# One Trainium2 core, a graph network: ScalarE's work on a tile put in another order

## The chip, the cores and the metric

The kernel runs on one core of one Trainium2 chip. The metric is the device time of one execution in microseconds (us). Before the change it was 12189.33 us, the median of 3 runs (12188.68 to 12192.55).

## The reference, cut to what matters

Four graph layers run over 6250 nodes of 128 features with 206,250 directed edges (self loops among them): a graph attention layer made of two attention convolutions, a neighbour sum, a transformer-like attention and an edge network. The change touches the two attention convolutions (4 heads of 32) of the first layer:

```python
h = (x @ W).reshape(N, H, C)
e = leaky_relu(alpha_s[src] + alpha_d[dst], 0.2)
e_exp = exp(e - segment_max(e, dst)[dst])
alpha = e_exp / (segment_sum(e_exp, dst)[dst] + 1e-16)
out = segment_sum(h[src] * alpha[:, :, None], dst)
...
feat_neigh = segment_sum(edge_val[:, None] * feat_in[edge_col], edge_row)   # second layer
```

The neighbour sum of the second layer is computed as a dense matrix product. That dense matrix of edge weights is written to DRAM beside the two convolutions, half of its columns in each.

## The kernel before, in words

**Nodes and units.** The nodes are sorted by falling degree into 49 tiles of 128, and the tiles into NB = 7 bands of B7 = 7. The edges into a band are cut into units. A unit is S = 2 edge slots for each of the band's 7 x 128 nodes, so 14 gathers of 128 table rows. Empty slots gather one and the same dummy row. The program has 130 units in all. A band has between 15 and 29 of them, and `k.beside` deals them out to its seven tiles.

**The attention pass** (`attention_pass`) is called three times: twice by `gat_conv` (called pass 1 and pass 2 here), and once for the later attention layer, without the dense rows. Its engines are these:

- POOL issues the gathers (L818) into a ring of RU = 4 units. Before a unit it claims `used` (the ring place is free again) and, before every second unit, the index that SP loads (L832).
- SP tells DVE by `landed` that a unit has arrived, and loads the next index once two units have arrived.
- DVE takes a unit in `unit`: scores (L1289, L1291), the running maximum (L1136), the difference `x` (L1137) with `e_ready`. It then waits for `p_ready`, multiplies the gathered rows by the exponentials (L1143 twice, where the second frees the ring place), rescales the sum (L1147) and adds (L1150, L1151).
- ScalarE answers each `e_ready` with the exponential (L1205) and a copy of the maximum (L1207).

**The dense rows** (`DenseRows`, in pass 1 and pass 2 only) are built tile by tile between the units. A tile has two phases, and in this program each phase has one chunk (`nch` is 1 everywhere). In a phase, DVE writes two sets of 16 one-hot blocks of 128x128 (L937, L939) from a small fetched column `col`. ScalarE first issues the fetch of the column for later use (`act_fetch`, L969, two DMAs) and then multiplies the 16 blocks `hot_lo` by the edge weights (L993). PE multiplies the pairs into four PSUM banks (L961), which it has cleared before with a product of zeros (L954). PE increments `full` when a phase is done. ScalarE's `act_store` waits for `full` and for `stage_out` (its store before has landed), copies the four banks to SBUF (L1004), giving each back to PE by `bank_free`, and issues two DMAs of 512 KB to DRAM (L1008). There is one set of four banks, so PE's products of phase 1 begin after the copies of phase 0.

**Order of DVE's work on a tile:** phase 0, phase 1, in pass 2 one step of the sums below, then the tile's units (2 to 5), and at the end of a band the division and, in pass 2, a layer norm.

**Sums over sources** (`SourceSums`, pass 2 only, from the second band on): the dense rows of the band before are read back in 14 parts of 1568 KB (`act_load`, L1042, two per tile, issued by ScalarE as the first thing of a tile and each only when `mat_free` says that PE is done with the buffer), multiplied by PE (`pe_step`, L1054, two groups of 7 products per tile, after the tile's second phase) and added by DVE (L1064, `dve_step`).

**Order of ScalarE's work on a tile, before:** the two loads (pass 2), phase 0, store 0, phase 1, all exponentials of the tile, store 1.

Of the kernel before, what the change touches and what calls it, by code (L numbers as in the profile page):

```python
# [15 lines left out]
ALU = mybir.AluOpType  # L16
ACT = mybir.ActivationFunctionType
AX = mybir.AxisListType
RMAX = bass.bass_isa.ReduceOp.max
ds = bass.ds  # L20
# [3 lines left out]
E = 206250  # L24
# [5 lines left out]
B7 = 7  # L30
NB = T // B7
W7 = B7 * P
S = 2
# [4 lines left out]
CROWS = EROWS + 16  # L38
DCOLS = 256
DROWS = -(-E // DCOLS)  # L40
UMAX = E // S + 256
SCOLS = UMAX * UG + 8 * CH * B7
SPARTS = ((0, 44), (44, 88), (88, P))
TROWS = 2 * EROWS + T + 16
# [144 lines left out]
def order_nodes(k, dst_rows, dst_firsts):  # L189
# [3 lines left out]
    with ExitStack() as st:  # L193
# [22 lines left out]
        band, bcnt, run = (s.sb(n, [P, NB]) for n in ("band", "bcnt", "run"))  # L216
        bi = s.sb("bi", [P, NB], I32)
# [47 lines left out]
        def _(dve):  # L265
# [86 lines left out]

            c(dve.tensor_scalar(bi[:, :], band[:, :], float(S - 1), None, ALU.add))
            c(dve.tensor_single_scalar(bi[:, :], bi[:, :], 1, ALU.arith_shift_right))
            c(dve.tensor_scalar(bcnt[:, :], bi[:, :], float(B7), None, ALU.max))
            c(dve.tensor_tensor_scan(run[:, :], k.ones[:, 0:NB], bcnt[:, :], 0.0, ALU.mult, ALU.add))
            c(dve.tensor_scalar(ti[:, 0:1], run[:, NB - 1:NB], 1.0, None, ALU.add))
            c(dve.tensor_single_scalar(ti[:, 0:1], ti[:, 0:1], 2, ALU.arith_shift_right))
# [512 lines left out]


def band_units(k, eng, b):
    return eng.value_load(k.units[0:1, ds(b, 1)], min_val=B7, max_val=UMAX)


def band_start(k, eng, b):
# [190 lines left out]
def attention_pass(k, table, slot_src, width, heads, dim, scores, start, finish, extra, beside=None, spill=None,  # L1068
# [6 lines left out]
    with ExitStack() as st:  # L1075
# [45 lines left out]
        def _(dve):  # L1121
# [32 lines left out]
            def band(b, before):  # L1154
                start(dve, c, b * B7, acc, e[:, S, :], work, second)
                c.reset()
                u0 = band_start(k, dve, b)
                if rows_of is None:
                    with dve.Fori(u0, u0 + band_units(k, dve, b)) as u:
                        unit(u)  # L1160
                else:
                    run.put(u0)
                    for w in range(B7):
                        rows_of.dve_tile(dve, rows_of.chunks(dve, b * B7 + w))
                        if before and w:
                            by_source.dve_step(dve, w - 1)
                        many = dve.value_load(k.beside[0:1, ds(b * B7 + w, 1)], min_val=1, max_val=UMAX)
                        u = run.value()
                        with dve.Fori(u, u + many) as v:
                            unit(v)  # L1170
                        run.advance(many)
                if before:
                    by_source.dve_step(dve, B7 - 1)
                c(dve.drain())

                a4 = acc[:, :, :].rearrange("p w (h c) -> p (w h) c", h=heads)
                c(dve.tensor_scalar(rden[:, :], a4[:, :, dim], 1e-16, None, ALU.add))
                c(dve.reciprocal(rden[:, :], rden[:, :]))
                done = k.out[:, ds(b * B7, B7), :] if by_source is None else by_source.xs[:, :, :]
                c(dve.tensor_tensor(done.rearrange("p w (h c) -> p (w h) c", h=heads),  # L1180
                                    a4[:, :, 0:dim], rden[:, :].unsqueeze(2).broadcast_to([P, HW, dim]), ALU.mult))
                finish(dve, c, b * B7, done, by_source)
                c.reset()
# [13 lines left out]
        @block.scalar  # L1197
        def _(act):
            act.activation(warm[:, :], k.ones[:, 0:1], ACT.Exp)

            def exponents(n):
                with act.Fori(0, n):
                    act.wait_ge(e_ready, 1)
                    act.sem_clear(e_ready)
                    act.activation(p, x[:, :, :], ACT.Exp)  # L1205

                    act.activation(e[:, S, :], newmax[:, :], ACT.Copy).then_inc(p_ready, 1)  # L1207

            def band(b, before):
                for w in range(B7):  # L1210
                    t = b * B7 + w
                    if before:
                        if w == 0:
                            act.wait_ge(rows_of.stage_out, 32)
                        by_source.act_load(act, b - 1, w)
                    n = rows_of.chunks(act, t)
                    for u in range(rows_of.PHASES):
                        rows_of.act_phase(act, t, u, n)
                        if u < rows_of.PHASES - 1:
                            rows_of.act_store(act, t, u)  # L1220
                    exponents(act.value_load(k.beside[0:1, ds(t, 1)], min_val=1, max_val=UMAX))
                    rows_of.act_store(act, t, rows_of.PHASES - 1)

            if rows_of is None:
                exponents(act.value_load(k.total[0:1, 0:1], min_val=2, max_val=UMAX))
            else:
                rows_of.act_begin(act, spill)
                if by_source is None:
                    with act.Fori(0, NB) as b:
                        band(b, False)  # L1230
                else:
                    band(0, False)
                    with act.Fori(1, NB) as b:
                        band(b, True)
                rows_of.act_end(act)
                if by_source is not None:
                    for w in range(B7):
                        by_source.act_load(act, NB - 1, w)
# [1413 lines left out]
```

## Time and profile before

| | us |
|---|---|
| median of 3 runs | 12189.33 |
| the profiled execution's own time | 12168.16 |
| its span, first to last instruction | 12166.3 |
| pass 1, first dense-row work to the last unit | 418 to 2826 |
| pass 2, likewise | 2954 to 5634 |
| third attention pass | 5998 to 8320 |

Engines overlap, so their busy shares don't add up to the span. A wait "for DVEq" or "POOLq" means that the engine's own sequencer held it: it stood at a semaphore or ran control instructions. "issue" is a gap with no wait that the trace shows. An "x16" in a timeline joins that many instructions of a kind that follow each other.

### The profile page before, as it was taken

Reading aid. Unit: us, or ns where it says so; the run is one execution under the profiler, and the core shown is the slowest. Engines: PE = TensorE matmul, PEld = TensorE weight load, DVE = VectorE, ACT = ScalarE, POOL = GpSimd, SP = SyncE. Lnnn points to the kernel's source line nnn. Section 1 sums busy time; section 2 is a strip of 40 time slices with the busy share of each in tenths; the row PEclk is TensorE's granted clock in tenths of the full one; section 3 lists DMA queues with packets and bytes.
Section 4 is the critical chain, followed back from the end, with each engine's and each line's share of the span. In section 5 each row is a group of like instructions: output and inputs, shape, how many; then the busy total and the mean of one; then the engine's idle time right before and its main releaser. Section 6 shows DMA issues by size and latency. Waiting matters only on the chain. (4 is left out here: it accounts for less than half of the span.)

```text
span 12166.3 us, 91441 instructions
## 1 busy us (share of the span) xinstructions
PE 3704.8 (30%) x14114; PEld 2564.3 (21%) x14213; DVE 6446.5 (53%) x10684; ACT 2415.0 (20%) x6031; POOL 7481.0 (61%) x7840
## 2 busy tenths in 40 slices
PE   2212233332224555555200000003311111113987
PEld 2212222322113333333200000001211111112433
DVE  6445666664545665563655666665332222223877
ACT  1112333331212233221100000000000000001876
POOL 4676777774767766552576777772276777774023
PEclk7556666665557777778655555556655555556999
DMA  2255444443375665555247444442137333334866
GB/s 59 68 76 92 101 107 108 114 109 58 89 102 150 167 163 160 151 156 144 75 111 103 112 112 112 112 112 35 40 103 92 104 104 107 104 107 122 280 243 214
DMA packets 928552, 1422.94 MB, mean 117 GB/s; under 512 B 191108, under 2 KB 723306, under 8 KB 927992
## 3 DMA queue, kind: packets, MB, share of 16 engines
q0 software_dynamic: 277904, 662.94, 26.4%
q10 hardware_dynamic: 549664, 498.96, 14.4%
q1 hardware_dynamic: 100680, 257.93, 6.3%
q14 instruction: 229, 1.88, 0.0%
q8 instruction: 75, 1.23, 0.0%
HBM read 1064.18 MB, written 355.03 MB: 117 GB/s over the span
## 5 line engine op out<-in xcount | busy, mean ns | idle before, releaser
L818 POOL DMA_INDIRECT ring<-gat_table,index x3640 | 3470.8, 954 | 1536.9 <-issue 1054.2
L818 POOL DMA_INDIRECT ring<-b_table,index x1820 | 1730.2, 951 | 671.0 <-issue 526.0
L818 POOL DMA_INDIRECT ring<-kv_table,index x1820 | 1722.8, 947 | 594.6 <-issue 526.1
L961 PE MATMUL pairs<-hot_lo,hot_hi 128*128 128x128 f32 x6272 | 1173.9, 373 | 1845.9 <-PEq L959 1845.9
L961 PEld LDWEIGHTS pairs<-hot_lo,hot_hi 128*128 128x128 f32 x6272 | 1142.3, 286 | 1922.0 <-issue 1922.0
L993 ACT ACTIVATE hot_lo<-hot_lo,wt 128x128 f32<-128x128 f32 x3136 | 949.4, 387 | 1895.4 <-ACTq L991 1881.5
L1911 DVE TENSOR_TENSOR tb<-bt,att 128x1792 f32 x130 | 263.2, 2025 | 1661.7 <-DVEq L106 1661.7
L1143 DVE TENSOR_TENSOR first<-ring,first 128x924 f32<-128x924 f32 x260 | 292.5, 1125 | 1495.6 <-DVEq L106 1495.6
L1933 PE MATMUL bt<-ident,ring 128*128 128x128 f32 x1820 | 417.2, 421 | 1932.0 <-PEq L106 1932.0
L2066 ACT ACTIVATE r<-kept_ring,coef 128x448 f32<-128x448 f32 x1040 | 763.8, 758 | 184.9 <-ACTq L106 161.0
L713 PE MATMUL tp<-ident,stage 128*128 128x128 f32 x196 | 49.0, 427 | 2444.7 <-DVEq L700 2410.5
L1933 PEld LDWEIGHTS bt<-ident,ring 128*128 128x128 f32 x1820 | 370.2, 226 | 1979.2 <-issue 1979.2
L1744 DVE TENSOR_TENSOR ring<-ring,qt 128x1904 f32 x130 | 277.9, 2138 | 786.5 <-DVEq L106 786.5
L954 PE MATMUL pairs<-nil 128*128 128x512 bf16 x686 | 277.5, 439 | 1317.6 <-PEq L106 1283.9
L1054 PE MATMUL fsum<-layer_out,xs 128*128 128x448 f32 x1372 | 540.6, 546 | 71.8 <-PEq L1052 70.2
L937 DVE TENSOR_TENSOR hot_hi<-hi,ramp 128x512 f32<-128x512 f32 x784 | 542.7, 692 | 29.4 <-DVE hi L931 3.2
L713 PEld LDWEIGHTS tp<-ident,stage 128*128 128x128 f32 x196 | 37.9, 222 | 2456.0 <-issue 2456.0
L939 DVE TENSOR_TENSOR hot_lo<-lo,ramp 128x512 f32<-128x512 f32 x784 | 550.1, 702 | 0.0
L2369 POOL TENSOR_SCALAR lift<-fnt,coef,bound 128x896 f32<-128x896 f32 x7 | 23.5, 3361 | 767.7 <-issue 518.6
L1205 ACT ACTIVATE p<-x 128x168 f32<-128x168 f32 x130 | 40.8, 314 | 2261.5 <-DVE x L1137 2261.5
L2020 ACT ACTIVATE v<-v,ep 128x1 f32<-128x1 f32 x2 | 0.6, 294 | 2392.5 <-DVEq L2013 2392.5
L1004 ACT ACTIVATE dstage<-pairs 128x512 f32<-128x512 f32 x784 | 404.8, 602 | 327.6 <-ACTq L1002 327.6
(414 smaller groups left out, 7926.4 us busy)
## 6 DMA issues: line engine op xcount, KB each, us to landing
kept_ring<-kept SPq DMA_DIRECT2D x260, 896.0 KB, 4.6
dense_weights<-dstage ACTq DMA_DIRECT2D x392, 512.0 KB
layer_out<-dense_weights ACTq DMA_DIRECT2D x98, 1568.0 KB, 14.8
kept<-tb ACTq DMA_DIRECT2D x132, 896.0 KB, 3.8
ring<-gat_table,index POOLq DMA_INDIRECT x3640
ring<-kv_table,index POOLq DMA_INDIRECT x1820
ring<-b_table,index POOLq DMA_INDIRECT x1820
col<-turned ACTq DMA_DIRECT2D x400, 32.0 KB
```

The lines of the kernel that those rows point to most:

```text
L818: pool.indirect_dma_start(self.ring[:, r * UG + i, :], None, self.table, bass.IndirectOffsetOnAxis(self.index[:, half, at:at + 1], 0)).the ...
L937: dve.tensor_tensor(self.hot_hi[:, u, four, :], self.hi[:, four].unsqueeze(2).broadcast_to(shape), ramp, ALU.is_equal)
L939: dve.tensor_tensor(self.hot_lo[:, u, four, :], self.lo[:, four].unsqueeze(2).broadcast_to(shape), ramp, ALU.is_equal).then_inc(self.marke ...
L954: pe.matmul(self.ps[:, b, :], self.nil[:, 0:P], self.nil[:, :], start=True, stop=False, skip_group_check=True)
L961: mm = pe.matmul(self.ps[:, b, i * P:(i + 1) * P], self.hot_hi[:, u, 4 * b + i, :], self.hot_lo[:, u, 4 * b + i, :], start=False, stop=Fal ...
L993: last = act.activation(self.hot_lo[:, u, j, :], self.hot_lo[:, u, j, :], ACT.Copy, scale=self.wt[:, u, j:j + 1])
L1004: act.activation(self.stage[:, 4 * b:4 * b + 4, :].rearrange("p i c -> p (i c)"), self.ps[:, b, :], ACT.Copy).then_inc(self.bank_free[b], 1)
L1054: mm = pe.matmul(self.ps[:, u, 0:BLK], self.xs[:, j, :], self.mat[:, u, j, :], start=(j == 0), stop=(j == B7 - 1))
L1143: ins = dve.tensor_tensor(by_head(dst), by_head(got[:, part, 0:VB]), weight[:, part, :].unsqueeze(3).broadcast_to([P, B7, heads, dim + 1]) ...
L1744: return (lambda: dve.tensor_tensor(keys4, keys4, qt[:, :, :].unsqueeze(1).broadcast_to([P, S, B7, VB]), ALU.mult), lambda: dve.tensor_red ...
L1933: mm = pe.transpose(bt[:, r % 2, q, w * P:(w + 1) * P], ga.ring[:, r * UG + q * B7 + w, :], k.ident[:, :])
L2066: act.activation(self.r4[:, q, :], self.slots[:, r, q * QW:(q + 1) * QW], ACT.Relu, bias=self.coef[:, 1:2], scale=self.coef[:, 0:1]).then_ ...
```

## The change

ScalarE now does, for a tile: the two loads (pass 2), phase 0, phase 1, one exponential, store 0, the other exponentials, store 1. Since the exponential is now once outside of the loop and the rest inside, every tile must have at least two units, so the floor of a band's units goes from 7 to 14. The smallest band has 15 units in the trace, and the total stays 130. UMAX, a bound for allocation, grows by 256.

```diff
-UMAX = E // S + 256
+UMAX = E // S + 512
...
-            c(dve.tensor_scalar(bcnt[:, :], bi[:, :], float(B7), None, ALU.max))
+            c(dve.tensor_scalar(bcnt[:, :], bi[:, :], float(2 * B7), None, ALU.max))
...
-            def exponents(n):
-                with act.Fori(0, n):
-                    act.wait_ge(e_ready, 1)
-                    act.sem_clear(e_ready)
-                    act.activation(p, x[:, :, :], ACT.Exp)
-
-                    act.activation(e[:, S, :], newmax[:, :], ACT.Copy).then_inc(p_ready, 1)
+            def exponent():
+                act.wait_ge(e_ready, 1)
+                act.sem_clear(e_ready)
+                act.activation(p, x[:, :, :], ACT.Exp)
+
+                act.activation(e[:, S, :], newmax[:, :], ACT.Copy).then_inc(p_ready, 1)
...
                     for u in range(rows_of.PHASES):
                         rows_of.act_phase(act, t, u, n)
-                        if u < rows_of.PHASES - 1:
-                            rows_of.act_store(act, t, u)
-                    exponents(act.value_load(k.beside[0:1, ds(t, 1)], min_val=1, max_val=UMAX))
-                    rows_of.act_store(act, t, rows_of.PHASES - 1)
+                    exponent()
+                    rows_of.act_store(act, t, 0)
+                    many = act.value_load(k.beside[0:1, ds(t, 1)], min_val=2, max_val=UMAX)
+                    with act.Fori(1, many):
+                        exponent()
+                    rows_of.act_store(act, t, 1)
```

The value bounds of two other loads are adapted to the new floor.

## Rows read from the trace of the kernel before

**Rows 1.** The page, group of the gathers of pass 1 and pass 2

```profile
L818 POOL DMA_INDIRECT ring<-gat_table,index x3640 | 3470.8, 954 | 1536.9 <-issue 1054.2
```

**Rows 2.** Waits of POOL (total, times, longest), 1972 to 2826 us (pass 1)

```profile
POOL ring L818 <- issue: 180.0, 588, 1.1
POOL ring L818 <- POOLq L106: 26.9, 39, 4.6
```

**Rows 3.** Waits of POOL, 3549 to 5634 us (pass 2, after its first gather-heavy band)

```profile
POOL ring L818 <- POOLq L106: 297.5, 67, 24.6
```

**Rows 4.** Timeline (start, length, instruction, idle before), DVE: last waits for a gather

```profile
1954.62 0.22 DVE L1289 TENSOR_TENSOR es<-ring,ad 128x56 f32<-128x56 f32 x1 [7.39 <-DVEq L106]
...
3525.13 0.22 DVE L1289 TENSOR_TENSOR es<-ring,ad 128x56 f32<-128x56 f32 x1 [1.38 <-DVEq L106]
```

**Rows 5.** Timeline, ScalarE, a tile of two units in pass 2

```profile
4685.24 0.22 ACT L1205 ACTIVATE first<-x 128x84 f32<-128x84 f32 x1
...
4692.85 2.06 ACT L1004 ACTIVATE dstage<-pairs 128x512 f32<-128x512 f32 x4
...
4707.27 4.78 ACT L993 ACTIVATE hot_lo<-hot_lo,wt 128x128 f32<-128x128 f32 x16 [12.36 <-ACTq L991]
...
4717.69 1.57 ACTq L1008 DMA_DIRECT2D dense_weights<-dstage  x2
4720.93 2.67 ACTq L969 DMA_DIRECT2D col<-turned  x2
4723.74 4.78 ACT L993 ACTIVATE hot_lo<-hot_lo,wt 128x128 f32<-128x128 f32 x16 [6.26 <-ACTq L991]
4728.43 0.22 ACT L1205 ACTIVATE first<-x 128x84 f32<-128x84 f32 x1
```

**Rows 6.** Timeline, PE, the same tile

```profile
4694.45 5.50 PE L1054 MATMUL fsum<-layer_out,xs 128*128 128x448 f32 x14 [0.41 <-PEq L1052]
...
4716.15 1.84 PE L954 MATMUL pairs<-nil 128*128 128x512 bf16 x4 [1.01 <-PEq L106]
4725.16 6.74 PE L961 MATMUL pairs<-hot_lo,hot_hi 128*128 128x128 f32 x32 [7.16 <-PEq L959]
```

**Rows 7.** Windows (busy per engine, then PEclk, DMA share, GB/s): that product's start

```profile
4725.00:4728.00 3.00, 2.84 (x13) 2.87 (x14) 0.00 (x0) 3.00 (x12) 0.00 (x0) 0.50 0.22 74
```

**Rows 8.** DMA traffic, 4716 to 4732 us in 40 slices of 0.4 us

```profile
GB/s 44 0 98 76 0 65 109 49 178 179 164 175 164 189 140 270 298 246 228 184 200 280 308 261 127 16 0 0 0 0 8 12 14 2 0 0 0 0 0 0
```

**Rows 9.** Timeline, ScalarE, a tile of three units in pass 2

```profile
4772.53 0.22 ACT L1205 ACTIVATE first<-x 128x84 f32<-128x84 f32 x1
...
4787.36 2.06 ACT L1004 ACTIVATE dstage<-pairs 128x512 f32<-128x512 f32 x4
...
4802.08 4.79 ACT L993 ACTIVATE hot_lo<-hot_lo,wt 128x128 f32<-128x128 f32 x16 [12.65 <-ACTq L991]
...
4822.10 0.22 ACT L1205 ACTIVATE first<-x 128x84 f32<-128x84 f32 x1
```

**Rows 10.** Timeline, ScalarE, first exponentials of two tiles in pass 1, two units between them

```profile
1545.25 0.22 ACT L1205 ACTIVATE first<-x 128x84 f32<-128x84 f32 x1
...
1582.70 0.22 ACT L1205 ACTIVATE first<-x 128x84 f32<-128x84 f32 x1
```

**Rows 11.** Timeline, ScalarE and POOL, end of the first band in pass 1

```profile
904.87 4.78 ACT L993 ACTIVATE hot_lo<-hot_lo,wt 128x128 f32<-128x128 f32 x16 [46.10 <-ACTq L991]
946.22 2.07 ACT L1004 ACTIVATE dstage<-pairs 128x512 f32<-128x512 f32 x4 [36.57 <-ACTq L1002]
...
959.36 0.22 ACT L1205 ACTIVATE first<-x 128x84 f32<-128x84 f32 x1
...
962.90 0.94 POOL L818 DMA_INDIRECT ring<-gat_table,index  x1 [39.93 <-POOLq L106]
```

**Rows 12.** Timeline, SP and DVE, end of pass 1

```profile
2791.67 1.07 SPq L832 DMA_DIRECT2D index<-slot_src  x3
...
2824.45 1.12 DVE L1151 TENSOR_TENSOR acc<-first,acc 128x924 f32<-128x924 f32 x1
```

More of the change, by code:

```diff
@@ L873, in band_units @@
 def band_units(k, eng, b):
-    return eng.value_load(k.units[0:1, ds(b, 1)], min_val=B7, max_val=UMAX)
+    return eng.value_load(k.units[0:1, ds(b, 1)], min_val=2 * B7, max_val=UMAX)
 def band_start(k, eng, b):
@@ L1166, in band @@
                             by_source.dve_step(dve, w - 1)
-                        many = dve.value_load(k.beside[0:1, ds(b * B7 + w, 1)], min_val=1, max_val=UMAX)
+                        many = dve.value_load(k.beside[0:1, ds(b * B7 + w, 1)], min_val=2, max_val=UMAX)
                         u = run.value()
@@ L1218, in band @@
                         rows_of.act_phase(act, t, u, n)
-                        if u < rows_of.PHASES - 1:
-                            rows_of.act_store(act, t, u)
-                    exponents(act.value_load(k.beside[0:1, ds(t, 1)], min_val=1, max_val=UMAX))
-                    rows_of.act_store(act, t, rows_of.PHASES - 1)
+                    exponent()
[4 more added lines that the diff above has]
+                    rows_of.act_store(act, t, 1)
             if rows_of is None:
-                exponents(act.value_load(k.total[0:1, 0:1], min_val=2, max_val=UMAX))
+                with act.Fori(0, act.value_load(k.total[0:1, 0:1], min_val=2, max_val=UMAX)):
+                    exponent()
             else:
```

## The prediction

> **What bounds the kernel now.** I read the page first, then windows and waits for each attention pass, then the timelines of the engines. The page names POOL: 3640 gathers of 954 ns in pass 1 and pass 2 [rows 1]. With the 0.31 us that follow each (180.0 over 588, [rows 2]) a gather costs 1.26 us, a unit of 14 gathers 17.6 us, and that is POOL's pace: 35.3 us for a tile of two units, 52.9 for three. Averages hide who is last, so the next question is who waits for whom. DVE waits for a gather for the last time at 1954.62 in pass 1, and at 3525.13 in pass 2 [rows 4]. From there to the end of either pass (2826 and 5634) the gathers are there before DVE wants them, and POOL waits for DVE: 26.9 us in the last three bands of pass 1, 297.5 us in pass 2 from 3549 on, the usual 0.31 us each included [rows 2, 3]. So 850 us of pass 1 and 2085 us of pass 2 are not set by POOL. The third pass has no dense rows and is not touched.
>
> What DVE waits for there is the tile's first exponential. DVE is ready for it some 10 us early in pass 1 and 13 to 16 us in pass 2, since ScalarE comes to it only after store 0 and phase 1. I call its start T. From T to T a tile of two units takes 37.45 us in pass 1 [rows 10] and 43.19 us in pass 2 [rows 5], one of three units in pass 2 49.57 us [rows 9]. POOL would need 35.3 and 52.9. In pass 2 the 36 steps between tiles of one band from 3549 on divide into 20 of two units (mean 43.2), 10 of three (mean 50.3) and 6 in which a DMA issue of ScalarE is held up (48.8 to 61.8), so the rows shown are typical.
>
> **The direct effect.** Between the end of phase 0's blocks (4707.27 + 4.78 = 4712.05) and the start of phase 1's (4723.74) ScalarE spends 11.69 us: it waits for PE, copies four banks, issues the store and then the fetch [rows 5]. After the change what stays is the control code before the fetch (4720.93 less the store's end 4719.26: 1.67), the fetch 2.67 and 0.14 more: 4.48 us. The first exponential comes 7.21 us earlier after the same start of phase 0. Nothing else is removed. The two store DMAs, the copies and the second fetch are all still issued, and the code of one more exponential per tile costs no time that the rows show.
>
> **Pass 1, the pace.** The loop there runs from T over DVE's two units (about 15 us) to the next phase 0 and back: 37.45 less 7.21 is 30.2. ScalarE's own loop is now longer, because PE begins phase 1's products only after the copies: copies at T + 0.4, zeros done at T + 3.0 (the copies begin 0.74 us before the first zeros, which take 1.84, [rows 6]), products until T + 9.9 (below), copies of store 1 until T + 13, its DMAs until T + 15, control code 1.7. So phase 0's fetch starts at T + 17 instead of T + 15 (1560.24 by the timeline), and the loop is 32.5 us. That is under POOL's 35.3, so POOL's gathers become the bound of pass 1. Its end moves: POOL loses its waits (26.9 less 39 x 0.31 = 14.8 us), so the last index load, which follows the landing of the last units, goes from 2791.67 to 2777 [rows 12]. DVE then needs about 8 us for the last unit and is done at 2785 instead of 2825.57: **40 us** gained. The bounds are 0 (the loop stays over 35.3) and 54 (the landing itself, held up by gathers of the dummy row, comes earlier still).
>
> **The end of the first band.** Gathers of the dummy row fill the DMA engines there. Store 0 waits until 946.22 for the landing of the store before, the first exponential comes at 959.36, and POOL stands 39.93 us until 962.90 [rows 11]. After the change the exponential doesn't wait for that landing. With 4.48 us between the phases it comes at about 909.65 + 4.48 + 4.7 = 919. But store 0 is then next, and the second exponential stands behind it until 946.22 + 2.07 + 1.57 + 1.7 = 951.6. The ring place of the first unit comes free in time and that of the second at 954. POOL, which also needs an index that lands late, gains about 20 us, and DVE, whose five units end about 8 us after a chain that starts at 951.6 instead of 959.97 plus one unit, gains about 15. Low bound 8 (the fetch is blocked until 946 as well), high 27. Pass 1 follows POOL: **20**. Pass 2 has the same event and follows DVE: **15**.
>
> **Pass 2, the pace.** Here PE closes a second loop. Its step of the sums comes after phase 1's products, and the second load of the next tile, which stands ahead of phase 0 on ScalarE, waits for the end of that step. Before, the step ended at 4699.95 and phase 0's blocks began 7.32 us later, T + 22.03 [rows 5, 6]. After: zeros done at T + 3.0, 0.3 for the loop's start, products 6.6, then 0.4 + 5.5 + 0.4 + 5.5 for the two groups of the step: T + 21.7, and phase 0's blocks at T + 29.0. From there to T again it was 43.19 - 22.03 = 21.16 and is now 13.95. The loop is **42.95 us** where it was 43.2: of the 7.2 us, 7.0 are given back. In a tile of three units ScalarE was held by the third exponential anyway (copies at T + 14.83, blocks at T + 29.55, [rows 9]) and PE is done by T + 21.7, so nothing is given back and 50.3 becomes about 43. The first tile of a band starts from DVE, and gains 7.2 less 0.5, since the last step of the band before now ends 1 us later.
>
> Sum: 20 x 0.25 = 5; 10 x 7.3 = 73; 6 x 6.7 = 40; the six held steps 15 (one of three units, one with a store issue in front of the exponential): **130 us** (133 rounded). POOL's 297.5 us of waits show that it can follow.
>
> The products' 6.6 us are the least certain. They took 6.74 at the lower clock level of 1.2 GHz (granted 0.50, [rows 7]), with PE idle for 7.16 us before [rows 6], but paced by ScalarE. All blocks now stand ready. At the lower level I keep near that row; the bound below is half of it, 3.4 us, at 2.4 GHz. The Trainium skill, "TensorE: Matmul & The Clock Gate", section "HAM oscillation — how this bites in real kernels", says that a PE which idles between bursts starts each burst at the lower clock; that speaks for the long value and against the change, and this trace agrees with 0.50. By it the sum stays as it is.
>
> Store 1's copies wait for store 0's landing. Traffic ends at about 4726.4, 8.7 us after the issue at 4717.69 [rows 8], so it lands at T + 11.4, and the loads are ready before T + 21.7 all the same. A landing of over 13 us would lengthen the loop.
>
> **Sum.** 40 + 20 + 15 + 130 = 205 us. The profiled execution's own time is 12168.16, 21 us under the median, and would be 11963. The median goes from 12189.33 to **11985 us**.
>
> **Rivals.**
> - *PE comes up early.* Phase 1's products run at the upper clock level, right behind the zeros. The loop of pass 2 is 3.3 us shorter in 33 steps: 109 us more, **11876**. For it: the products now join the step in one run. Against: 7 us of idling before. 15 in 100.
> - *More is given back.* Store 0 and store 1 are 9 us apart instead of 18, and the loads follow at once; DMA issues stall ScalarE as in the six held steps. 2 us more in 33 steps and half of the 40 us lost at the end of pass 1: 86 us less, **12070**. 18 in 100.
> - *The gathers are the bound.* POOL is the busiest engine; if all waits of DVE are slack the time stays at **12189**. Against: no wait for a gather after 1954.62 and 3525.13. 7 in 100.
> - *Slower.* The second exponential now stands behind store 0. ScalarE is free at T + 0.4 + 2.1 + 0.2 + 1.6 + 1.7 = 6.0 and DVE asks at T + 7.0, so there is 1 us of room. A store that stalled 5 us, by a landing or a full queue, would cost 4 us in each of the 63 tiles that DVE or ScalarE sets: 252 less 205, **12236**. From 4.3 us on it eats the gain. Against: the landing in 8.7 us. 5 in 100.
>
> **Numbers.** The forecast has 55 in 100, with 11930 to 12035 as its own range. The range over the first three is 11865 to 12095. A difference under 0.2% (24 us) can hardly be told from none. Faster by more: 0.88; within: 0.07; slower: 0.05.
>
> **What would show it.** In pass 1, DVE's waits for gathers (L1289) come back after 1954 and the wait ahead of L1143 turns into them; the last unit ends some 60 us earlier. In pass 2 the distance between first exponentials is near 43 in tiles of two and of three units alike, ScalarE's second load starts at about T + 22, and the products of phase 1 take 6 to 7 us right behind the zeros. If that distance is below 40, PE was sized wrongly; if above 45, the loads or stores stall; if store 0 starts late, the second exponential moves with it.

## The result and the profile after

The changed kernel takes **11841.72 us** (median of 4 runs, 11837.08 to 11864.19) beside 12189.01 us of the kernel before (4 runs, 12181.88 to 12192.55). The ratio is 0.9719, its 95% interval 0.9703 to 0.9736: 2.8% faster, where 1.7% was forecast. The time lies 23 us under the low end of the range. The profiled execution took 11864.19 us and its span is 11862.3, 304.0 less than the span before. It was the slowest of its four, 22 us over their median, and the one before lay 21 us under its median, so the traces show some 43 us less of a difference than the medians. In lines of the changed kernel the exponential is L1204 (L1205 before), the copy behind it L1206 (L1207) and the first read of a gathered unit L1291 (L1289); the variants below move these and other lines by up to five more.

I read first how long POOL was held at its gathers in the whole program, because the gathers were the busiest group and the forecast left them with slack. The columns are the total in us, the number of waits and the longest. Before:

```profile
POOL ring L818 <- POOLq L106: 695.6, 406, 78.1
```

After:

```profile
POOL ring L818 <- POOLq L106: 368.6, 409, 78.0
```

Nearly the same number of waits lasts 327 us less, and the saving is 347 us: what was won is for the most part the time that POOL had stood still. The page after, groups of POOL and DVE in pass 1 and pass 2:

```profile
L818 POOL DMA_INDIRECT ring<-gat_table,index x3640 | 3477.4, 955 | 1204.2 <-issue 1046.9
...
L1143 DVE TENSOR_TENSOR first<-ring,first 128x924 f32<-128x924 f32 x260 | 292.6, 1126 | 559.6 <-DVEq L106 552.7
...
L1291 DVE TENSOR_TENSOR es<-ring,ad 128x56 f32<-128x56 f32 x260 | 56.1, 216 | 947.3 <-DVEq L106 947.3
```

The same two groups of DVE before:

```profile
L1143 DVE TENSOR_TENSOR first<-ring,first 128x924 f32<-128x924 f32 x260 | 292.5, 1125 | 1495.6 <-DVEq L106 1495.6
...
L1289 DVE TENSOR_TENSOR es<-ring,ad 128x56 f32<-128x56 f32 x260 | 57.0, 219 | 326.4 <-DVEq L106 326.4
```

DVE's wait for the exponential (ahead of L1143) fell from 1495.6 to 559.6 us, and its wait for a gathered unit rose from 326.4 to 947.3. A gather costs what it did (955 ns, 954 in [rows 1]), and its idle time fell from 1536.9 to 1204.2. Of what is left, 1046.9 stands under "issue", the 0.3 us behind each gather. Pass 2 after its first gather-heavy band shows it most clearly. Waits of POOL, 3494 to 5302 us, the stretch that was 3549 to 5634 before:

```profile
POOL ring L818 <- POOLq L106: 19.5, 64, 0.3
```

Of 297.5 us [rows 3] 19.5 are left, and no wait is longer than 0.3 us. One line of the view that groups instructions, POOL, 3494 to 5230 us:

```profile
L818 POOL DMA_INDIRECT ring<-gat_table,index x1378 | 1315.8, 955 | 420.2 <-issue 400.7 <-POOLq L106 19.5
```

Busy and idle time add up to the whole 1736 us: 1378 gathers at 1.26 us each, one behind the other. The issue of the gathers is now the bound of pass 2 from 3494 to POOL's last gather at 5234. The 67 us from there to the end of the pass are not POOL's: they belong to the last units, of which more below. DVE tells the same from the other side, in pass 2 (3494 to 5320 us):

```profile
DVE first L1143 <- DVEq L106: 291.6, 99, 24.0
DVE es L1291 <- DVEq L106: 140.0, 20, 14.7
```

and in pass 1 (1958 to 2770 us):

```profile
DVE es L1291 <- DVEq L106: 172.6, 22, 17.2
DVE first L1143 <- DVEq L106: 42.2, 45, 2.3
```

L1291 is the wait for a gathered unit. Before, there was none in the like stretches (behind 1954.62 and 3525.13, [rows 4]). In pass 1 the wait for the exponential (L1143) has shrunk to 2.3 us at most, from up to 22.1 before. The last unit of pass 1 begins its product at

```profile
2771.26 1.13 DVE L1143 TENSOR_TENSOR first<-ring,first 128x924 f32<-128x924 f32 x1 [0.74 <-DVEq L106]
```

in the timeline after and is finished 5.5 us later, at 2776.8, where it was 2825.57 [rows 12]: 48.8 us. The last unit of pass 2 ends at 5302.0, where it was 5632.9: 330.9 us. So pass 2 itself gave 282 us. Three parts make it up, read by taking the same gather in both traces. The end of the first band put POOL 17 us ahead (46.7 us ahead of the old kernel in front of it, 63.7 behind it). From there to POOL's last gather (5580.35 before, 5233.77 now) it won 283 us, of which its waits are 278 (297.5 less 19.5). Behind the last gather some 16 us were lost again: the pass ended 51.6 us after it before and ends 67.3 us after it now.

**One tile of two units in pass 2.** The timeline of ScalarE, beside [rows 5]:

```profile
4826.59 0.22 ACT L1204 ACTIVATE first<-x 128x84 f32<-128x84 f32 x1
...
4826.87 2.02 ACT L1004 ACTIVATE dstage<-pairs 128x512 f32<-128x512 f32 x4
4829.10 1.57 ACTq L1008 DMA_DIRECT2D dense_weights<-dstage  x2
4833.74 0.24 ACT L1204 ACTIVATE first<-x 128x84 f32<-128x84 f32 x1 [4.86 <-DVE x L1137]
...
4837.27 2.06 ACT L1004 ACTIVATE dstage<-pairs 128x512 f32<-128x512 f32 x4 [3.14 <-ACTq L1002]
4839.53 1.42 ACTq L1008 DMA_DIRECT2D dense_weights<-dstage  x2
4841.38 6.28 ACTq L1042 DMA_DIRECT2D layer_out<-dense_weights  x2
4849.28 3.40 ACTq L969 DMA_DIRECT2D col<-turned  x2
4852.82 2.44 ACT L993 ACTIVATE hot_lo<-hot_lo,wt 128x128 f32<-128x128 f32 x8 [13.49 <-ACTq L991]
4855.17 0.48 ACTq L969 DMA_DIRECT2D col<-turned  x1
...
4855.74 0.56 ACTq L969 DMA_DIRECT2D col<-turned  x1
4855.76 6.53 ACT L993 ACTIVATE hot_lo<-hot_lo,wt 128x128 f32<-128x128 f32 x22
4862.18 0.24 ACT L1204 ACTIVATE first<-x 128x84 f32<-128x84 f32 x1
```

From T to T it is 35.59 us, not 42.95. The reader should look at L969 near 4855: the fetch for phase 1 is issued while the blocks of phase 0 still run, and there is no gap between the 16 blocks of one phase and those of the other. The first exponential comes 9.36 us after the start of phase 0 (4852.82 to 4862.18), not 13.95. So it is in nearly all tiles of pass 2 from the second band on, but for the first of each band. In most tiles of pass 1 it is 11.23 us: there the second 16 blocks start 1.37 us behind the first, because DVE has only just written its first set of phase 1 (ready at 1547.89, ScalarE starts at 1548.03). PE beside it [rows 6]:

```profile
4827.58 2.02 PE L954 MATMUL pairs<-nil 128*128 128x512 bf16 x4 [2.87 <-PEq L106]
4829.40 5.77 PE L961 MATMUL pairs<-hot_lo,hot_hi 128*128 128x128 f32 x32
4835.58 5.50 PE L1054 MATMUL fsum<-layer_out,xs 128*128 128x448 f32 x14 [0.41 <-PEq L1052]
4841.48 5.50 PE L1054 MATMUL fsum<-layer_out,xs 128*128 128x448 f32 x14 [0.41 <-PEq L1052]
```

The step ends at T + 20.4 (forecast 21.7), and the blocks follow 5.84 us later (forecast 7.32). PE's clock during the zeros and the products, in windows (the granted clock is the column before the DMA share):

```profile
4827.50:4829.40 1.90, 1.82 (x4) 0.55 (x5) 1.90 (x3) 1.38 (x3) 1.60 (x2) 0.50 0.32 73
4829.40:4831.40 2.00, 2.00 (x11) 2.00 (x11) 1.97 (x2) 0.00 (x0) 1.39 (x3) 0.50 0.50 114
...
4833.40:4835.20 1.80, 1.77 (x15) 1.58 (x13) 1.06 (x2) 0.39 (x2) 1.32 (x2) 0.94 0.97 252
```

Zeros and products begin at 1.2 GHz (0.50) after 2.87 us without work; until 4826.5 the granted clock had been 1.00. The last products run near 2.4 GHz (0.94).

**The end of the first band in pass 1**, timeline of ScalarE, beside [rows 11]:

```profile
869.32 33.09 ACTq L969 DMA_DIRECT2D col<-turned  x2
902.55 2.44 ACT L993 ACTIVATE hot_lo<-hot_lo,wt 128x128 f32<-128x128 f32 x8 [39.62 <-ACTq L991]
...
915.02 0.22 ACT L1204 ACTIVATE first<-x 128x84 f32<-128x84 f32 x1
...
949.34 2.07 ACT L1004 ACTIVATE dstage<-pairs 128x512 f32<-128x512 f32 x4 [33.95 <-ACTq L1002]
951.61 4.34 ACTq L1008 DMA_DIRECT2D dense_weights<-dstage  x2
956.75 0.24 ACT L1204 ACTIVATE first<-x 128x84 f32<-128x84 f32 x1 [5.34 <-DMA raw<-in_edges_dram,rid]
```

The first exponential no longer waits for the landing (915.02, before 959.36), and the second does: it stands behind store 0 until 956.75. Later, in the sixth tile of the last band of pass 2, a store's issue itself took long:

```profile
5207.71 26.99 ACTq L1008 DMA_DIRECT2D dense_weights<-dstage  x2
5235.49 0.24 ACT L1204 ACTIVATE first<-x 128x84 f32<-128x84 f32 x1 [27.99 <-DMA raw<-in_edges_dram,rid]
```

From T to T this tile takes 76.4 us, where it took 52.3 before. The tile ahead of it had been held before (59.7 us, by a store's issue of 11.06 and a fetch of 8.86) and takes 37.6 now, so over both tiles the loss is 2 us (114.0 beside 112.0). Such a hold can still cost time there, because it lasts past POOL's last gather at 5234. The releaser in brackets, a DMA long past, is only inferred; what ended just before the exponential is the store's issue, ahead of it in ScalarE's order.

### The profile page after: what moved, and what is told of

It is laid out like the page before. It is cut to its first block and busy times, and to the rows that moved or that the text cites. A ratio compares the mean times of both kernels' runs of the same rounds, so it can differ in the third digit from the quotient of the medians.

```text
span 11862.3 us, 91343 instructions
## 1 busy us (share of the span) xinstructions
PE 3664.7 (31%) x14212; PEld 2474.3 (21%) x14213; DVE 6449.6 (54%) x10684; ACT 2409.2 (20%) x6031; POOL 7496.8 (63%) x7840
## 5 line engine op out<-in xcount | busy, mean ns | idle before, releaser
L818 POOL DMA_INDIRECT ring<-gat_table,index x3640 | 3477.4, 955 | 1204.2 <-issue 1046.9
L961 PE MATMUL pairs<-hot_lo,hot_hi 128*128 128x128 f32 x6272 | 1069.8, 350 | 997.7 <-PEq L959 981.9
L961 PEld LDWEIGHTS pairs<-hot_lo,hot_hi 128*128 128x128 f32 x6272 | 1049.9, 265 | 1059.9 <-issue 1049.2
L954 PE MATMUL pairs<-nil 128*128 128x512 bf16 x784 | 359.0, 531 | 1833.6 <-PEq L106 1753.1
L1143 DVE TENSOR_TENSOR first<-ring,first 128x924 f32<-128x924 f32 x260 | 292.6, 1126 | 559.6 <-DVEq L106 552.7
L1291 DVE TENSOR_TENSOR es<-ring,ad 128x56 f32<-128x56 f32 x260 | 56.1, 216 | 947.3 <-DVEq L106 947.3
L937 DVE TENSOR_TENSOR hot_hi<-hi,ramp 128x512 f32<-128x512 f32 x784 | 544.4, 694 | 29.4 <-DVE hi L931 3.2
L954 PEld LDWEIGHTS pairs<-nil 128*128 128x128 bf16 x784 | 80.2, 102 | 2072.7 <-issue 2067.2
L1204 ACT ACTIVATE p<-x 128x168 f32<-128x168 f32 x130 | 40.8, 314 | 2275.6 <-DVE x L1137 2275.6
```

What stands on the lines that cost most here:

```text
L818: pool.indirect_dma_start(self.ring[:, r * UG + i, :], None, self.table, bass.IndirectOffsetOnAxis(self.index[:, half, at:at + 1], 0)).the ...
L937: dve.tensor_tensor(self.hot_hi[:, u, four, :], self.hi[:, four].unsqueeze(2).broadcast_to(shape), ramp, ALU.is_equal)
L954: pe.matmul(self.ps[:, b, :], self.nil[:, 0:P], self.nil[:, :], start=True, stop=False, skip_group_check=True)
L961: mm = pe.matmul(self.ps[:, b, i * P:(i + 1) * P], self.hot_hi[:, u, 4 * b + i, :], self.hot_lo[:, u, 4 * b + i, :], start=False, stop=Fal ...
L1143: ins = dve.tensor_tensor(by_head(dst), by_head(got[:, part, 0:VB]), weight[:, part, :].unsqueeze(3).broadcast_to([P, B7, heads, dim + 1]) ...
```

## The experiments

All ratios are to the kernel before, timed on the same chip in the same series; 0.001 is 12 us.

| | median, us | ratio | 95% interval |
|---|---|---|---|
| the change | 11841.72 | 0.9719 | 0.9703 to 0.9736 |
| floor_only | 12195.99 | 1.0001 | 0.9992 to 1.0011 |
| pass1_only | 12115.68 | 0.9962 | 0.9949 to 0.9976 |
| pass2_only | 11889.29 | 0.9773 | 0.9760 to 0.9787 |
| drain_pass1 | 11841.40 | 0.9713 | 0.9697 to 0.9729 |
| drain_pass2 | 11878.51 | 0.9742 | 0.9725 to 0.9758 |
| store_first | 11910.54 | 0.9771 | 0.9755 to 0.9788 |
| short_step_old | 12138.11 | 0.9981 | 0.9971 to 0.9990 |
| short_step | 11802.59 | 0.9702 | 0.9686 to 0.9718 |
| split_loads | 11808.06 | 0.9710 | 0.9693 to 0.9726 |
| two_stages | 11811.54 | 0.9712 | 0.9698 to 0.9725 |
| two_stages_split | 11793.77 | 0.9696 | 0.9683 to 0.9709 |
| two_stages_short | 11790.05 | 0.9680 | 0.9667 to 0.9694 |

**floor_only**: the kernel before with the new floor of units and the new bounds alone.

```diff
-            c(dve.tensor_scalar(bcnt[:, :], bi[:, :], float(B7), None, ALU.max))
+            c(dve.tensor_scalar(bcnt[:, :], bi[:, :], float(2 * B7), None, ALU.max))
```

> The kernel before with nothing but the new floor of two units per tile and the larger bound UMAX. All theories: no tile changes its units, the time stays within 0.2% of 12189 us. Rival D: part of the gain is from another dealing of units, over 25 us faster.

No difference. The whole saving comes from the order of ScalarE's work.

**pass1_only** and **pass2_only**: the new order in one pass, the old one in the other.

```diff
+                    if by_source is None:        # pass2_only: is not None
                         (phases, exponential, store 0, exponentials, store 1)
+                    else:
+                        (phase 0, store 0, phase 1, exponentials, store 1)
```

> The new order in pass 1 alone; pass 2 keeps the old one. If the saving splits as the ends of the passes in the two profiled executions say (48 us by the end of pass 1, 283 more by the end of pass 2), the time is about 12141 us, ratio 0.996. If the passes are coupled (what pass 1 gains is lost in an unchanged pass 2, or the reverse), it is over 12170. By the sum of the prediction, 40 + 20 us, it would be 12129.

> The new order in pass 2 alone. By the ends of the passes: 283 to 300 us less, 11889 to 11906, ratio 0.9755. The two single savings should add up to that of the whole change (347 us). By the sum of the prediction, 130 + 15 us, it would be 12044.

Pass 1 gives 46 us (0.38% of 12189) and pass 2 gives 277 (2.27%), together 323 of the 343 that the ratio 0.9719 stands for; each of these has an interval of some 16 us to either side, so they add up within the noise. The ends of the passes in the traces had said 49 and 282 (283 in the expectation). The forecast had 60 and 145, so its error lies in pass 2.

**drain_pass2** and **drain_pass1**: ScalarE waits between the two phases until its blocks are written, so that nothing behind them is issued early.

```diff
                         rows_of.act_phase(act, t, u, n)
+                        if u == 0 and by_source is not None:        # drain_pass1: is None
+                            act.drain()
```

> The kernel after, with ScalarE told to drain between phase 0 and phase 1 in pass 2 alone. Theory A (the gap between the phases vanished: the control code and the fetch of phase 1 run under the blocks of phase 0, where 4.5 us were forecast): the gap comes back, the distance between first exponentials in pass 2 goes from 35.6 us to about 40 in tiles of two units, and the time from 11842 to 11970 to 12030 us. Rival B (the surplus came from PE's clock and the loads): at most 20 us slower, 11842 to 11862.

> The same drain in pass 1 alone. If the gathers set pass 1 now (35.3 us for two units, against a loop of some 29 us), 4.5 us more per tile are hidden but for the first tiles of bands and the overfull end of the first band: within 15 us of 11842. If ScalarE or DVE still set pass 1, 49 x 4.5 = 220 us slower, about 12060.

The timeline of ScalarE in drain_pass2:

```profile
4857.64 4.78 ACT L993 ACTIVATE hot_lo<-hot_lo,wt 128x128 f32<-128x128 f32 x16 [13.71 <-ACTq L991]
4863.43 1.12 ACTq L969 DMA_DIRECT2D col<-turned  x2
4864.69 4.78 ACT L993 ACTIVATE hot_lo<-hot_lo,wt 128x128 f32<-128x128 f32 x16 [2.27 <-ACTq L991]
```

The gap is 2.27 us, of which the fetch is 1.12, and this tile takes 38.3 us (4831.07 to 4869.38). So even with the overlap forbidden the gap is half of my 4.48: the fetch had taken 2.67 us right behind the two DMAs of store 0 [rows 5] and takes 1.12 here. Why it is shorter was not tested. The first five tiles of the sixth band take 36.8 us on average, 2.1 more than in the changed kernel and not the 40 that I had expected. The time fell between my two theories: I had expected at least 11970 us by one and at most 11862 by the other. By the ratios the drain costs 28 us, with intervals that overlap. Timed in one series with the drain in pass 1, it costs 37 us more than that one (11873.56 to 11889.60 beside 11839.69 to 11842.77), clear of noise. So the overlap is real, but it is the smaller part of the gain: with it forbidden in pass 2, the kernel still saves 314 of the 343 us. In pass 1 the drain changes nothing, as expected where the gathers are the bound.

**store_first**: both phases, then store 0, then all exponentials. It separates the two halves of the change.

```diff
-                    exponent()
                     rows_of.act_store(act, t, 0)
                     many = act.value_load(k.beside[0:1, ds(t, 1)], min_val=2, max_val=UMAX)
-                    with act.Fori(1, many):
+                    with act.Fori(0, many):
```

> Both phases, then store 0, then all exponentials of the tile, then store 1: the reordering of the phases without the exponential ahead of store 0. Theory A (in pass 2 ScalarE and PE set the pace in a loop that does not hold the exponential): tiles of pass 2 stay near 35.6 us, only the first exponential comes some 4 us later; 20 to 60 us slower than 11842, 11862 to 11900. Rival C (what counts is that DVE gets its first exponential before the store): most of the gain goes, above 12000 us.

Timeline of ScalarE in store_first:

```profile
4813.38 2.01 ACT L1004 ACTIVATE dstage<-pairs 128x512 f32<-128x512 f32 x4
...
4818.74 0.24 ACT L1204 ACTIVATE first<-x 128x84 f32<-128x84 f32 x1 [3.35 <-DMA raw<-in_edges_dram,rid]
```

The first exponential comes 5.3 us behind the last block, and the five tiles of two units in the sixth band take 36.3 to 37.6 us. Of the saving of 343 us, 279 remain: putting the phases together is worth about four fifths, and the one exponential ahead of store 0 the rest. That is 11 us more lost than my first theory allowed, and far from the 12000 of its rival.

**short_step** and **short_step_old**: the changed kernel and the one before, with one of the seven products in each group of the sums. Six sevenths of the sum are left out, the loads are kept.

```diff
-            for j in range(B7):
+            for j in range(1):
                 mm = pe.matmul(self.ps[:, u, 0:BLK], self.xs[:, j, :], self.mat[:, u, j, :], ...)
```

> The kernel after, in which each group of the sums over sources makes one product of seven (the rest of the sum is left out, the loads are all still there). Theory A (after the change the loop over PE's step and the second load sets pass 2): the step shrinks from 11.4 us to about 2, ScalarE waits for DVE or the gathers instead, tiles of two units go to DVE's 30 to 35 us or the gathers' 35.3, of three to 52.9 where a backlog allows less; pass 2 can give up to 60 us, 11780 to 11825. The last seven tiles' sums add 50 us at most. Rival E (ScalarE's own work sets it): no more than the tail's 50.

> The same omission in the kernel before. There the step should have set little, since the store of phase 0 and its wait stood in between: theory A: ScalarE's second load starts at once rather than at T + 15, some 3 us per tile of two units earlier, pass 2 60 to 100 us faster plus up to 50 from the tail of the sums: 12040 to 12130 us. Rival E: only the tail, 12140 to 12189.

Timeline of ScalarE in short_step:

```profile
4795.64 0.22 ACT L1204 ACTIVATE first<-x 128x84 f32<-128x84 f32 x1
...
4806.32 2.06 ACT L1004 ACTIVATE dstage<-pairs 128x512 f32<-128x512 f32 x4 [3.13 <-ACTq L1002]
...
4810.26 4.50 ACTq L1042 DMA_DIRECT2D layer_out<-dense_weights  x2
4816.40 3.96 ACTq L969 DMA_DIRECT2D col<-turned  x2
4820.50 2.44 ACT L993 ACTIVATE hot_lo<-hot_lo,wt 128x128 f32<-128x128 f32 x8 [12.12 <-ACTq L991]
```

PE's step shrinks from 11.4 to 2.4 us, and the tile still takes 34.2 us (next T at 4829.86). The copies of store 1 stand at T + 10.7 as before. PE's products were done at T + 7.9 (4798.45 + 5.08), so they wait for something else, and the only other thing is the landing of store 0. My statement that PE closes the loop of pass 2 was therefore half of the truth at best. The saving beside the full kernels is the same 0.2% in the new (0.9702 to 0.9719) and the old order (0.9981), so it doesn't come from the loop. The traces show where it comes from: the 14 groups of products left over behind the end of pass 2 run from 5315.36 to 5413.78 in the changed kernel and from 5314.46 to 5382.51 in short_step, 30 us less. For the kernel before I had expected 60 to 100 us from the loop, and that didn't come either.

**two_stages**: a staging buffer and a landing semaphore for each phase, so that store 1 doesn't wait for store 0. **two_stages_short**: the same, with short_step's omission.

```diff
-        self.stage = s.sb("dstage", [P, PP, P])
+        self.stage = s.sb("dstage", [P, 2, PP, P])
...
-        act.wait_ge(self.stage_out, 32)
-        act.sem_inc(self.stage_out, -32)
+        act.wait_ge(self.stage_out[u], 32)
+        act.sem_inc(self.stage_out[u], -32)
```

> The changed kernel with a staging buffer and a landing semaphore for each phase, so that the copies of store 1 no longer wait for the landing of store 0. Theory: PE's step of the sums, whose end the second load waits for, closes the loop in tiles of two units in pass 2, and the landing is 1.7 us behind it. Then the copies of store 1 go from 10.7 to about 9 us after the first exponential, the distance between first exponentials stays at 35 to 36.5 us, and only the end of the first band gains, since the second exponential there no longer stands behind a landing (956.75 goes to about 925): 10 to 30 us in all, 11812 to 11832. Rival: the landing closes the loop and the distance falls below 34.5, 20 to 30 us more. Second rival: two stores in flight share the DMA engines with gathers and loads, and the time is that of the changed kernel or above.

> Both suspects of the loop of pass 2 at once: a staging buffer for each phase, and one of the seven products in each group of the sums (the rest of the sum is left out, the loads are kept). Theory: two chains of nearly the same length close the loop in tiles of two units, PE's step (33.7 us with the landing gone) and the landing of store 0 (33.9 us with the step cut); with both gone ScalarE's own issues or DVE remain, 29 to 31 us. Rival: one cause stands behind both, the time of the loads' issues and landings, and the distance stays at 33 to 34. In the total either gives at most 30 us beyond the 11800 of two_stages_split, since the gathers are the bound of most of pass 2: 11770 to 11810 (ratio 0.967 to 0.971), 20 us of which come from the shorter tail of the sums.

The same five tiles of two units, at the head of the sixth band in pass 2, take on average:

| | us from T to T |
|---|---|
| the change | 34.7 |
| short_step (PE's step cut) | 34.6 |
| two_stages (no wait for the landing) | 33.4 |
| two_stages_short (both) | 31.6 |

One by one the two give 0.1 and 1.3 us, together 3.1. That is what two chains of nearly the same length do, and the rival of one common cause (33 to 34 us with both) is out, though 31.6 is also a little over the 29 to 31 that I had expected. With two_stages alone the distance fell below the 34.5 that I had named as the sign of the rival, that the landing closes the loop. In the total, two_stages stands 8 us under the change by the ratios, which can't be told from none. The timeline of ScalarE in two_stages shows the landing gone:

```profile
4820.52 2.06 ACT L1005 ACTIVATE dstage<-pairs 128x512 f32<-128x512 f32 x4 [0.63 <-ACTq L1003]
...
4836.71 2.44 ACT L994 ACTIVATE hot_lo<-hot_lo,wt 128x128 f32<-128x128 f32 x8 [14.13 <-ACTq L992]
```

The copies start at T + 8.2 (T is 4812.35), not T + 10.7. What closes the loop now is PE's step, which ends at T + 19.7 (4832.06), with the blocks 4.65 us behind it. Both parts were longer in the changed kernel (20.4 and 5.84): I had counted on neither shrinking when I expected 35 to 36.5 us. At the end of the first band in pass 1 the second buffer gave nothing:

```profile
921.74 42.00 ACTq L1009 DMA_DIRECT2D dense_weights<-dstage  x2
```

I had expected the second exponential at 925. The wait for the landing is gone, and the issue of the store stands 42 us in its place, with the second exponential behind it. The wait has only changed its place.

**split_loads**: the second load of the sums issued between the phases, so that the wait for PE's step is covered by phase 0. **two_stages_split**: the same with two staging buffers.

```diff
-                        by_source.act_load(act, b - 1, w)
+                        by_source.act_load(act, b - 1, w, (0,))
...
                         rows_of.act_phase(act, t, u, n)
+                        if u == 0 and before:
+                            by_source.act_load(act, b - 1, w, (1,))
```

> The kernel after with the tile's second load moved from ahead of phase 0 to between the phases (pass 2), so that phase 0 no longer waits for the end of PE's step. Theory A (that wait is now in the loop): the loop drops from 35.6 us to the gathers' 35.3 or DVE's 30 to 34; first exponentials come 3 to 5 us sooner in tiles of pass 2 and 10 to 60 us are gained, 11780 to 11830. Rival E: no change, or a loss where the later load keeps PE waiting, 11842 to 11900.

> As two_stages, and the second load of the sums issued between the two phases instead of ahead of both. Both known chains of the loop are shorter: the distance in tiles of two units in pass 2 falls to 27 to 30 us (30 to 31.4 with the moved load alone). If the gathers bound pass 2 by now, the total does not follow: within 15 us of two_stages. If ScalarE's chain were still the bound of the pass, 5 us in some 25 tiles would give another 100 us, 11710 to 11740.

The five tiles take 31.1 us in split_loads. In two_stages_split the first three take 29.4 us and the next two 34.2 (from 4834.1 on), since the gathers hold them. The total hardly follows: 0.9710 and 0.9696 beside 0.9719. I had expected two_stages_split within 15 us of two_stages, and it is 18 us faster. Where the time goes is seen in DVE's waits, 3494 to 5320 us, in split_loads

```profile
DVE es L1293 <- DVEq L106: 268.4, 38, 14.1
DVE first L1143 <- DVEq L106: 149.1, 98, 19.3
```

and in two_stages_split

```profile
DVE es L1296 <- DVEq L106: 293.5, 40, 13.6
DVE first L1145 <- DVEq L106: 109.9, 99, 19.4
```

From the change over split_loads to two_stages_split the wait for the exponential falls from 291.6 to 149.1 and 109.9 us, and the wait for the gathers rises from 140.0 to 268.4 and 293.5. The sum hardly moves: 432, 418, 403 us. If DVE's waits for the exponential were still the bound, 182 us less of them would have shown in the time; 28 us did, by the ratios. No run made the gathers cheaper: that they are the bound is read from POOL's waits and from these kernels, whose shorter tiles gave next to no time. Of all kernels that compute the whole result, two_stages_split is the fastest measured, 371 us under the kernel before by its ratio. Its interval touches that of the change (0.9709 and 0.9703), so that it beats the change is likely and not shown.

## Why the prediction was wrong

The direction and the first half of the mechanism held: DVE had waited for the first exponential, the phases together bring it earlier, and the gathers had room. The size was wrong, all of it in pass 2. The step that failed is the loop of a tile of two units there: 42.95 us by my sum, so that 7.0 of the 7.2 us would be given back, and 35.2 us measured. The terms of that loop come first.

- **Direct effect, 4.48 us left between the phases: the largest term of the loop that was wrong.** I took the control code (1.67), the fetch (2.67) and 0.14 from a place where ScalarE's engine was idle, and laid them between two phases, where 16 queued blocks hide them. 9.36 us instead of 13.95 make 4.6 us in a tile of pass 2 (2.7 in most tiles of pass 1, with 11.23). No bound stood on this term, though the row shows only how long that code takes in the open. drain_pass2 brings 2.27 us back, so the fetch had been taken too long as well, and it shows that this term alone doesn't explain the miss: even there 314 us are saved, where 205 were forecast.
- **The loop of two units in pass 2, 42.95 us: 35.6.** Besides those 4.6 us, the step's end came 1.3 us earlier (products 5.8 instead of 6.6, zeros 0.2 earlier, and none of the 0.3 for the loop's start) and the blocks behind it 1.5 us earlier (5.84 instead of 7.32). Together 7.4. The sentence "of the 7.2 us, 7.0 are given back" is the one that the term 20 x 0.25 = 5 hangs on. In truth nothing was given back: of the 25 steps of two units inside a band from 3494 on, 24 take 33.6 to 37.6 us, 35.2 on average, where the 20 undisturbed ones took 43.2. That is 8 us in each of 20, 160 where the sum had 5, and more than the whole miss of pass 2. For a distance below 40 I had written that PE was sized wrongly; PE's step is 1.3 of the 7.4 us, and ScalarE's own work the rest.
- **PE closes the loop: half right.** two_stages_short shows two chains, PE's step and the landing of store 0. I had put the landing at T + 11.4 with room to spare behind T + 21.7. It does not only have to be early enough for the loads to land: store 1's copies, its DMAs, two loads of 4.50 us and a fetch of 3.96 follow it, so a landing at T + 10.6 leads to blocks at T + 24.9 (short_step: 4795.64 to 4820.50).
- **Sum of pass 2, 130 + 15 us: 277 (pass2_only).** The missing bound was in [rows 3]. POOL's pace is 35.3 us for two units and 52.9 for three. With a loop at or under 35.3 POOL never waits, and then the gain is what POOL waited before: 297.5 less 67 x 0.31, that is 277 us. I used this row to say that POOL could follow, and did not ask what the time would be if it became the bound. That rival (12189 less 277 and less the 60 of pass 1) would have stood at 11852, or at 11837 with the 15 of pass 2's first band. The row gives the gain from 3549 to the last gather. That the whole pass came to the same 277 is luck in part: the 17 us of the first band's end and the 16 us lost behind the last gather cancel.
- **Pass 1, 40 + 20 us: 46.** Right in kind: the loop fell under POOL's pace, and the gathers are the bound. In the traces POOL stands 15 us ahead once the first band's end is past (the same gather at 1068.06 before and 1052.54 now), and the rest of the pass gives 33 of the 48.8, where I had 20 and 40. The same event in pass 2 gave POOL 17, where I had 15.
- **The first band's end.** The first exponential was forecast for 919 and came at 915.02, the second for 951.6 and came at 956.75: store 0's copies began at 949.34 and not at 946.22, and its issue took 4.34 us and not 1.57. That the second would stand behind the landing was right.
- **Rivals.** *PE comes up early* stood nearest with 11876, by the wrong road. The clock rose in the last third of the products (0.94 from 4833.4) and saved 0.8 us, not 3.3. The Trainium skill, "TensorE: Matmul & The Clock Gate", section "HAM oscillation — how this bites in real kernels", says that a PE which waits between bursts of matmuls starts the next one at the lower clock; the trace agrees, 0.50 after 2.87 us without work and 1.00 shortly before. What *Slower* describes, a second exponential held up behind store 0, is seen in the sixth tile of the last band (a store's issue of 26.99 us). The end of the pass lies 16 us later behind the last gather than before; how much of that is this store was not tested. *More is given back* fell. So did *The gathers are the bound*, which meant that they already were; that they would become it was no rival of mine.

## What to carry to other kernels

Time that control code and DMA issues take in the open is no term of a sum once the engine has queued work in front of them: put nothing and the full time as the two bounds. When a chain is shortened, work out first what the next bound allows. Here it was one row, the waits of the busiest engine: it said 277 us for the stretch where POOL waited, and 278 of its waits went, while the sum over chains missed the gain of the pass by half. Once that bound is reached, further shortening shows up as waits that move from one line to another, with their sum nearly the same.

## What was not expected of the hardware

- ScalarE's sequencer issues DMAs under its own engine's work: 0.48 and 0.56 us of L969 at 4855.17 and 4855.74, while blocks run from 4852.82 to 4862.29 without a gap.
- A DMA issue can hold an engine far longer than a transfer of its kind took elsewhere (8.7 us for two store DMAs, [rows 8]). While the DMA engines were busy, by the program with gathers of the one dummy row (DMA share 0.98 at 54 GB/s from 869 to 902), two fetch DMAs of 32 KB held ScalarE for 33.09 us (869.32), and with a second staging buffer two store DMAs held it for 42.00 (921.74), beside 1.57 us in a tile like that of [rows 5]. Busy DMA engines alone don't explain it: with a share of 1.05 at 379 GB/s (4816 to 4818) a fetch issue took 2.00 us. The cause was not tested. The Trainium skill, "DMA: Bandwidth & Descriptors", section "Issuing engines are not separate DMA queues", says that the time to initiate a DMA is usually small beside the DMA itself. The 1.57 us beside 8.7 agree; the 33.09 and 42.00 us at the ends of these bands don't.
